# Full attention core: one unit of first scores behind each pair of second-score units, in place of two behind the first pair

## The reference

```python
def _L1_attn_ref(x, Wq, Wk, Wv):
    DIM, HEADS = 128, 16
    HEAD_DIM = DIM // HEADS
    B, S, D = x.shape
    H, Hd = (HEADS, HEAD_DIM)
    q = (x @ Wq.T).reshape(B, S, H, Hd)
    k = (x @ Wk.T).reshape(B, S, H, Hd)
    v = (x @ Wv.T).reshape(B, S, H, Hd)
    energy = jnp.einsum('bqhd,bkhd->bhqk', q, k)
    attn = jax.nn.softmax(energy / jnp.sqrt(jnp.float32(D)), axis=-1)
    out = jnp.einsum('bhqk,bkhd->bqhd', attn, v).reshape(B, S, D)
    return out
```

## Time and profile before

| | us |
|---|---|
| median of 3 runs | 2973.12 |
| lowest and highest | 2971.78, 2983.54 |
| profiled execution | 2978.22 |
| its span | 2976.5 |
| PE busy (share of the span) | 2456.1 (83%) |
| DVE busy | 1900.8 (64%) |
| ACT busy | 1559.8 (52%) |
| POOL busy | 629.4 (21%) |

### The profile page before, as it was taken

One profiled execution on the slowest core, in us unless ns is written; L12 is line 12 of the kernel. 1 busy time (PEld: TensorE's weight loads), 2 busy tenths in 40 slices (PEclk: granted clock), 3 DMA queues, 4 the chain that ended last, 5 costly groups with the idle time before them and its releaser, 6 DMA issues. The chain is left out here.

```text
span 2976.5 us, 44274 instructions
## 1 busy us (share of the span) xinstructions
PE 2456.1 (83%) x15597; PEld 1151.8 (39%) x15642; DVE 1900.8 (64%) x2699; ACT 1559.8 (52%) x3161; POOL 629.4 (21%) x1182
## 2 busy tenths in 40 slices
PE   6986566899999999699978999998767877766668
PEld 3543343122222222267752333332446445544523
DVE  4544766898999996311137777772855485458577
ACT  2542452588888888433332666665455356442211
POOL 1760000000000000000010221221654084104256
PEclk7986786799999999899986999998889998987779
DMA  2210004211111110000001100100100000010000
GB/s 79 80 44 0 8 0 118 57 29 47 47 47 30 42 48 3 3 1 1 1 9 55 29 22 26 29 20 5 49 24 2 14 20 2 1 27 2 1 0 15
DMA packets 56251, 77.06 MB, mean 26 GB/s; under 512 B 23368, under 2 KB 35691, under 8 KB 56032
## 3 DMA queue, kind: packets, MB, share of 16 engines
q1 hardware_dynamic: 48384, 69.73, 8.4%
q10 hardware_dynamic: 7648, 4.50, 0.7%
HBM read 59.49 MB, written 10.49 MB: 24 GB/s over the span
## 5 line engine op out<-in xcount | busy, mean ns | idle before, releaser
L861 DVE TENSOR_REDUCE l1a_core_mpart<-l1a_core_psA 128x1 f32<-128x1024 f32 x512 | 601.1, 1218 | 66.9 <-PE l1a_core_psA L778 66.9
L845 ACT ACTIVATE l1a_core_prob<-l1a_core_psB 128x512 f32<-128x512 f32 x1024 | 551.3, 596 | 128.9 <-PE l1a_core_psB L791 127.1
L1194 DVE TENSOR_REDUCE l2a_core_mpart<-l2a_core_psA 128x1 f32<-128x1024 f32 (+7 forms) x384 | 335.3, 908 | 106.7 <-PE l2a_core_psA L1096 59.8
L1174 ACT ACTIVATE l2a_core_prob<-l2a_core_psB 128x384 f32<-128x384 f32 (+3 forms) x656 | 301.7, 525 | 182.0 <-PE l2a_core_psB L1111 181.0
L802 PE MATMUL l1a_core_psV<-l1a_core_prob,l1a_core_vh 128*32 128x512 f32 x2048 | 273.6, 606 | 0.1
L791 PE MATMUL l1a_core_psB<-l1a_core_qh,l1a_core_kh 75*128 75x512 bf16 x640 | 193.6, 384 | 0.8 <-ACT l1a_core_prob L845 0.8
L1127 PE MATMUL l2a_core_psV<-l2a_core_prob,l2a_core_vh 128*32 128x128 f32 (+3 forms) x1856 | 188.9, 437 | 4.9 <-POOL l2a_core_prob L1050 3.2
L1949 DVE SCALAR_TENSOR_TENSOR X<-l1e_psO,W,X 128x128 f32<-128x128 f32 x128 | 36.0, 343 | 202.9 <-PE l1e_psO L1906 202.9
L1938 ACT ACTIVATE l1e_h<-l1e_psH,l1e_w_b 128x512 f32<-128x512 f32 x128 | 87.9, 687 | 137.4 <-PE l1e_psH L1899 137.4
L1050 POOL TENSOR_SCALAR_AFFINE_SELECT l2a_core_prob<-l2a_core_prob 128x128 f32<-128x128 f32 x256 | 74.0, 293 | 341.4 <-ACT l2a_core_prob L1174 338.9
L1906 PEld LDWEIGHTS l1e_psO<-l1e_w_w,l1e_h 128*128 128x128 f32 x1024 | 118.7, 192 | 13.4 <-issue 13.4
(11 more groups left out here) (698 smaller groups left out, 4521.6 us busy)
## 6 DMA issues: line engine op xcount, KB each, us to landing
l2f_tab<-in_rotary SPq DMA_DIRECT2D x32, 128.0 KB, 2.0
l0a_core_qh<-qparts SPq DMA_DIRECT2D x36, 96.0 KB
l0a_core_kh<-kparts SPq DMA_DIRECT2D x36, 96.0 KB
l1a_core_qa<-qparts SPq DMA_DIRECT2D x32, 96.0 KB
l1a_core_ka<-kparts SPq DMA_DIRECT2D x32, 96.0 KB
l1a_core_qh<-qparts SPq DMA_DIRECT2D x30, 96.0 KB
l1a_core_kh<-kparts SPq DMA_DIRECT2D x30, 96.0 KB
l2a_core_qh<-qparts SPq DMA_DIRECT2D x30, 96.0 KB
```

The source lines that it names most:

```text
L845: nc.scalar.activation(prob[u % (2 * PER_KB)][:], psB[u % 3][:], ACT.Exp, scale=scale).then_inc(b_exped, 1)
L861: nc.vector.tensor_reduce(mpart[:, n // 2, n % 2:n % 2 + 1], psA[i % 2][:], AX.X, ALU.max).then_inc(a_freed, 1)
L1174: nc.scalar.activation(prob[n % RING][:, 0:cols], psB[n % 3][:, 0:cols], ACT.Exp, scale=scale).then_inc(b_exped, 1)
L1194: ins = nc.vector.tensor_reduce(mpart[:, place, part:part + 1], psA[i % 2][:, lo * P:hi * P], AX.X, ALU.max)
```

## The change

The two units of first scores of one kb no longer stand together behind its first pair of second scores. One stands behind the first pair and one behind the second pair, in front of the values. The quota, up to which slots are issued, is counted in half steps. Nothing else is changed: the same instructions with the same waits, buffers and tiles, and no other engine's queue has another order.

```diff
             for h in range(H):
                 begin, end = done, group_end[min(h + 1, H - 1)]
                 for kb in range(NT):
-                    score(h, kb, 0)
-                    score(h, kb, 1)
-                    while done < min(end, begin + 2 * (kb + 1) + (turned_by[min(h + 1, H - 1)] - 1 < begin + 2 * (kb + 1))):
-                        fill_slot(done)
-                        done += 1
-                    score(h, kb, 2)
-                    score(h, kb, 3)
+                    for half in range(2):
+                        score(h, kb, 2 * half)
+                        score(h, kb, 2 * half + 1)
+                        quota = begin + 2 * kb + half + 1
+                        while done < min(end, quota + (turned_by[min(h + 1, H - 1)] - 1 < quota)):
+                            fill_slot(done)
+                            done += 1
                     if kb:
                         values(h, kb - 1)
                     elif h:
```

## The result

The changed kernel takes 3008.91 us (median of 4 runs, 3004.24 to 3012.14) against 2975.46 us for the kernel before (4 runs). The ratio is 1.0101, with a 95% interval of 1.0083 to 1.0119. That is slower. Run again in more rounds, the same kernel stood at 1.0071 (1.0052 to 1.0091), so its price is between 0.5% and 1.2%, and the profile says where in that range: 23.4 us, or 0.8%.

What follows compares the result with a forecast made beforehand. TensorE's order with four shape changes was taken to set the attention core's step; 21.2 + 2.8 - 1.4 - 0.1 = +22.5 us, rounded to 22, on 2973.12 gave 2995 us, range 2984 to 3008.

Steps and rivals of the forecast that it cites:

- One more change of shape per step: TensorE's kb step in the attention core: five changes instead of four, 2.71 us against 2.62, +0.09 us a step.
- A to V: Distance from a psA unit's start to the psV matmuls', unseen in the trace before; taken as 0.31 us, bounds 0.225 and 0.40.
- The 39 us: Alternative estimate for the added shape changes: 236 x 0.166 us from the skill page's matmul latency, in place of 21 us.
- 236 steps: Steps of heads 0 to 14 with the added shape change: 14 x 16 + 12, at 0.09 us each +21.2 us.
- The fourth B: A step's fourth psB matmul, at 1.08 us, falls exactly on the first exponential's limit; cost 0, bound 0.02 us.
- the rival in which it waits in every step: Fourth psB matmul waits for the first exponential each step, another 0.09 us, 21 us on top, 3016 us; chance 0.10.
- The copy: Step 1 after ScalarE's psV copy: fourth psB matmul waits 0.20 us longer in heads 1 to 14, +2.8 us.
- VectorE: Second psA unit's wait for VectorE reductions at the end of a head shrinks by 0.10 us a head, -1.4 us.
- The last turn: Last turn of the maxima, step 12 of head 14: TensorE arrives 0.09 us later and waits less, -0.1 us.
- The first steps of head 0: First three steps, at the lower clock with other waits; reason for rounding the sum from 22.5 down to 22 us.
- The rival with a free edge: The new distance from a psA unit to psV costs nothing: step 2.62 us, total 2974 us; chance 0.10.
- the one in which VectorE held the step: VectorE's reductions, not TensorE, bound the step, so the spread-out order is faster: 2953 us; chance 0.03.

Runs made afterwards that it cites:

- six_changes: Kernel before with one psA unit behind the first and one behind the third psB matmul, six shape changes a step; step 2.82 us, ratio 1.0141.
- full_rows pair: Two kernels, full_rows_pairs and full_rows_split, with psA matmuls on all 128 rows, in the order of before and of the changed kernel; both steps 2.83 us.
- five_no_gate: Kernel before with one psA unit behind each psB pair, values between the pairs, psV copy behind the second exponential; step 2.72 us, ratio 1.0134.
- split_copy_later: Changed kernel with the psV copy behind a head's fifth exponential, not its fourth; core 702.51 us, ratio 1.0100 against the kernel before.
- full_rows_pairs: Kernel before, same order, with psA matmuls on all 128 rows, one behind the other; step 2.83 us, core 725.67 us, ratio 1.0159.
- full_rows_split: Changed kernel's order with psA matmuls on all 128 rows, one behind the other; step 2.83 us, core 732.95 us, ratio 1.0178 against the kernel before.
- three_changes: Kernel before with all four psB matmuls together, then both psA units and the values, three shape changes; step 2.94 us, ratio 1.0259.
- four_values_between: Kernel before with values between the psB pairs, both psA units behind the second pair, psV copy behind the second exponential; step 2.62 us, ratio 1.0029.

## Why the prediction was right

The prediction was 2995 us, 22 over the kernel before, with a range of 2984 to 3008. The ratio of 1.0101 on the 2973.12 us from which it was worked out is 3003 us, the repeated 1.0071 is 2994; the bare medians are 3009, just over the range, and 3005. The direction and the mechanism were right; the sum came closer than its terms did. Point by point:

1. *One more change of shape per step.* Right, and shown by six_changes and by the full_rows pair. The step came to 2.72 where I had 2.71, so the change costs 0.10 us over 2.62 and not 0.09. A to V was 0.32 (I took 0.31). The Trainium skill, TensorEngine Tiling (Array Packing), under Key Properties, says that a change of mode drains TensorE; the runs agree, with 0.32 against 0.22 us, and go on agreeing when the change of mode is taken away. The 39 us that I estimated from the Trainium skill's page TensorE: Matmul & The Clock Gate, under Single matmul latency, is too much: the core gained 23.4.
2. *236 steps.* 236 x 0.10 = 23.6 us, where I had 21.2.
3. *The fourth B.* It falls on the limit as worked out (weight load 0.05 behind the exponential), and costs nothing that can be told: five_no_gate has the same 2.72. So the rival in which it waits in every step, at 3016 us, didn't come.
4. *The copy.* +0.20 in heads 1 to 14 as foreseen (2.91 against 2.72), 2.7 us, and gone when the copy is moved.
5. *VectorE.* The wait of the second A is gone. A head got back 0.15 us where I had 0.10: the step in front of the turn went from 2.69 to 2.72 and the one with the turn from 2.83 to 2.84, not by 0.10 each. That is 2.1 us against 1.4. The second A comes 0.64 us later within the step (1.40 against 0.76 behind the first B), and not about 1.1 as I wrote; nothing in the sum hung on it.
6. *The last turn.* That step went from 3.98 to 3.88 us, 0.1 less as said.
7. *The first steps of head 0*, which I set aside with a rounding of half a us. The first four took 13.39 us against 13.85, so 0.5 less instead of 0.4 more, at a granted clock of 0.70 against 0.66.

The sum was +22.5 us for the core, and the core gained 23.4. The terms as measured are 23.6 + 2.7 - 2.1 - 0.1 - 0.9 (head 0, against 0.4 more) = 23.2. The price of a change was 2.4 us too small in all, and points 5 and 7 gave back 1.6 more than I had: that the two sums lie 1 us apart is in part luck.

What was off is the time as a whole. I took for granted that the rest of the kernel stays the same to a few us, and in the first measurement it was 7 us (by the ratio) to 10 us (by the medians) longer, in the second not at all. Of these 10, 4 are on the side of the changed kernel, whose median was 3008.91 and then 3004.97, and 6 on the side of the kernel before: 2975.46 in its first 4 runs, 2981.71 in the 17 beside the second measurement. Why, stays open: the starts of the core spread over 10 us in code that is the same in eight of the ten kernels.

The rival with a free edge fell at once (A to V is 0.32), and so did the one in which VectorE held the step: the second A no longer waits for it, and the step is longer.

No order of the ones tried beats the kernel before. It has four changes of shape, the fewest among these that leave each fourth B covered. A fourth psB buffer, with which three changes could perhaps go without the wait, wasn't tried; psA, psB and psV hold 4096 fp32 columns of PSUM already (2 x 1024, 3 x 512 and 512), and nothing here shows room for more.

## What to carry to other kernels

Count the changes of the array's shape around a loop, not the matmuls alone: rows show them as a longer distance between starts (0.32 against 0.22 us here, at 2.4 GHz and 512 columns, the only case shown) where nothing was waited for, and each lone product between others of another shape costs two. Take the shape from these distances, since rows of 75 and of 128 followed one another here without a gap. Work of one shape belongs together as far as its buffers allow, and no further: the four B in a row saved one change and paid 0.4 us for an exponential. When an edit touches one stage, measure that stage, and look at its granted clock first. The core's length repeated to 0.05 us where the clock was the same, and was 7 us off in split_copy_later where it wasn't; single executions of the whole kernel before spread over 18 us (2973.94 to 2991.77).

## What the hardware showed beside it

In five of the ten profiles the granted clock fell right behind the last turn of the maxima, in head 14, where no psA units are left: in full_rows_pairs, full_rows_split, three_changes and split_copy_later, and for only 3.4 us in five_no_gate. Windows of split_copy_later, TensorE's granted clock in the third column from the end, and two rows of its PE, the turn and the first step at the lower clock:

```profile
1150.00:1190.00 40.00, 38.90 (x231) 9.36 (x227) 34.26 (x32) 30.49 (x59) 0.75 (x4) 1.00 0.02 3
1190.00:1215.00 25.00, 24.14 (x87) 4.17 (x87) 0.22 (x1) 14.93 (x29) 0.37 (x2) 0.59 0.02 4
1215.00:1245.00 30.00, 26.83 (x157) 5.82 (x160) 0.00 (x0) 25.88 (x51) 0.00 (x0) 1.00 0.00 1
```

```profile
1190.60 0.22 PE L769 MATMUL l1a_core_psA<-identb,l1a_core_mb 128*128 128x128 bf16 x1 [1.70 <-POOL l1a_core_mb L741]
...
1192.29 1.91 PE L791 MATMUL l1a_core_psB<-l1a_core_qh,l1a_core_kh 75*128 75x512 bf16 x4
```

It was 1.00 (2.4 GHz) up to there and 0.59 on average over the 25 us from 1190, most of which is the lower level, 0.50 (1.2 GHz). Five steps of four B and V took 3.70 us in place of 2.40, and a sixth 2.76, 7 us in all. In full_rows_pairs two took 3.70, in three_changes and full_rows_split six. The kernel before, the changed kernel, its repetition and six_changes went through the same steps at full clock, 2.40 each, and four_values_between at full clock too, in its order's 2.56.

What TensorE did before it fell is much the same in all of them. In the four with a long fall PE had been idle for 1.49 to 1.70 us up to the matmul that turns the maxima, and the clock fell 1.0 to 1.5 us behind it; in five_no_gate PE had been idle for 2.42 us. But in the five that kept the full clock it had been idle for 1.59 to 1.80 us. So the idle time doesn't tell them apart. The four long falls are all four profiles taken on chip 3, and of the four taken on chip 0 only five_no_gate had one; for the first two profiles, of the kernel before and the changed one, the chip isn't known. Whether it is the chip, the kernel or chance the runs don't show: no kernel is known to have been profiled on both. The 7 us are a third of what this change costs.
